# Attention turned on VectorE in 32x32 blocks, and its softmax moved behind the low part of u

## The reference, cut to what matters

```
out    = (q k^T * scale) v              # per head; no softmax over keys here
out    = softmax(out, axis=-1)          # over the 8 channels of a head
x      = x + concat_heads(out) @ wo^T + wo_b
t      = rms_norm(layer_norm(x))        # tokens for the experts
w      = top-2 of 8 experts, from softmax(t @ gate^T)
h1, h3 = t @ w1^T + lora1_e, t @ w3^T + lora3_e     # base shared, LoRA per expert, rank 16
act    = silu(h1) * h3
x      = x + sum_e w_e * (act @ w2^T + lora2_e)
```

## Time and profile before

| | us |
|---|---|
| three timed runs | 297.27, 297.6, 298.34; median 297.6 |
| span of the profiled execution, first to last instruction | 296.7 |
| between that span and the median | 0.9 |

### The profile page before, as it was taken

How to read it: one execution, slowest core, us unless ns; L and a number is a source line. 1 busy time by engine, 2 the same in 40 slices (tenths; PEclk the granted TensorE clock), 3 DMA queues, 4 the chain that set the end, 5 groups by cost and what they waited for, 6 DMA issues and landing times. The chain is left out here.

```text
span 296.7 us, 4518 instructions
## 1 busy us (share of the span) xinstructions
PE 287.4 (97%) x1487; PEld 238.4 (80%) x1487; DVE 221.4 (75%) x607; ACT 187.5 (63%) x310; POOL 187.0 (63%) x186
## 2 busy tenths in 40 slices
PE   8779999999999999999999999999999999999995
PEld 6557888878888888888888888888888887878874
DVE  3878986995689658894589765895579965795295
ACT  1467967674945966757755868459656658655532
POOL 3375599288970889419990589608982389518930
PEclk9979999999999999999999999999999999999999
DMA  5720020200220021200211011200012000200002
GB/s 147 287 66 9 0 73 1 72 1 11 97 73 0 0 72 38 71 1 2 71 50 60 0 49 59 71 0 2 1 37 73 0 0 35 75 1 0 0 2 71
DMA packets 7225, 12.45 MB, mean 42 GB/s; under 512 B 1825, under 2 KB 3234, under 8 KB 7202
## 3 DMA queue, kind: packets, MB, share of 16 engines
q1 hardware_dynamic: 6768, 11.77, 12.0%
q10 hardware_dynamic: 434, 0.39, 0.4%
HBM read 10.03 MB, written 2.13 MB: 41 GB/s over the span
## 5 line engine op out<-in xcount | busy, mean ns | idle before, releaser
L989 ACT ACTIVATE silu<-h_ps 128x512 f32<-128x512 f32 x64 | 37.4, 596 | 31.4 <-PE h_ps L641 29.8
L1639 POOL TENSOR_TENSOR um_lo<-umf,um_hi 128x1024 fp32r<-128x1024 f32 x7 | 16.9, 2414 | 60.5 <-ACT um_hi L981 60.5
L641 PE MATMUL h_ps<-um_hi,b_hi 128*128 128x512 f32 x128 | 51.4, 401 | 0.0
L641 PE MATMUL h_ps<-um_lo,b_hi 128*128 128x512 f32 x128 | 50.3, 393 | 0.5 <-DVE um_lo L1309 0.5
L641 PE MATMUL h_ps<-um_hi,b_lo 128*128 128x512 f32 x128 | 49.9, 390 | 0.0
L1322 DVE TENSOR_TENSOR act_first<-silu,h_ps 128x512 f32<-128x512 f32 x32 | 21.4, 680 | 20.9 <-ACT silu L989 16.1
L1322 DVE TENSOR_TENSOR act_second<-silu,h_ps 128x512 f32<-128x512 f32 x32 | 21.7, 679 | 16.6 <-PE h_ps L641 14.7
L1661 POOL TENSOR_TENSOR scaled<-act_second,ratio 128x512 f32<-128x512 f32 x24 | 31.5, 1313 | 1.3 <-DVE act_second L1322 1.3
L641 PEld LDWEIGHTS h_ps<-um_lo,b_hi 128*128 128x128 f32 x128 | 24.0, 188 | 6.9 <-DVE um_lo L1309 1.4
L981 ACT CAST um_hi<-umf 128x1024 fp32r<-128x1024 f32 x14 | 14.8, 1055 | 23.2 <-DVE umf L1303 22.2
L641 PEld LDWEIGHTS h_ps<-um_hi,b_lo 128*128 128x128 f32 x128 | 24.1, 188 | 4.5
(11 more groups left out here) (278 smaller groups left out, 789.2 us busy)
## 6 DMA issues: line engine op xcount, KB each, us to landing
chosen<-choice_dram SPq DMA_DIRECT2D x7, 512.0 KB, 3.6
x_in<-in_x_dram SPq DMA_DIRECT2D x7, 256.0 KB, 2.9
ctx_in<-in_ctx_t_dram SPq DMA_DIRECT2D x7, 256.0 KB, 3.2
out_dram<-y SPq DMA_DIRECT2D x7, 256.0 KB, 2.0
act_second<-in_hidden_w_dram SPq DMA_DIRECT2D x1, 512.0 KB, 4.1
act_second<-in_lora_w_dram SPq DMA_DIRECT2D x1, 512.0 KB, 5.6
v_parts<-in_down_w_dram SPq DMA_DIRECT2D x1, 512.0 KB, 5.3
ctx_in<-in_ctx_t_dram ACTq DMA_DIRECT2D x2, 128.0 KB, 3.2
```

Source lines behind the costliest of these rows:

```text
L641: mm = nc.tensor.matmul((h1_ps, h3_ps)[s][n % 2][:], b13[w][:, s, c * P:(c + 1) * P], um[k][m][:, s, :], start=False, stop=(i == 2), skip_ ...
L989: nc.scalar.activation(silu[:, n % SILU_RING, :], h1_ps[n % 2][:], ACT.Silu).then_inc(silu_done.sem, 1)
L1639: nc.gpsimd.tensor_tensor(um[1][1][:], umf[1][:], as_f32(um[1][0][:]), ALU.subtract)\
```

## The change

For the blocks n >= 2 (`AHEAD` = 2):

- `attention_out` swaps the operands of its matmuls, so that `b_ps` holds channels (heads) on partitions and tokens along the row.
- DVE's new `turn_o(n)` transposes each 32x32 square of `b_ps` into `heads` (SBUF); a group of 8 columns is then one head of one token. It stands where `top_of_o` and `shift_o` stood.
- `top_of_o` and `shift_o` read `heads` instead of PSUM and stand later: behind `um_low(b+1)` and `v_part(b, 0)`. `sum_exp` follows `v_part(b, 1)`.
- DVE's new `turn_heads(n)` transposes the 32x32 squares of `heads` back into `heads_t`, at the head of the next iteration, in front of `act_step(b, 0)`. PE's `turn_heads` and ACT's `heads_turned` go.
- ACT: `exp_o` stands behind `exp_ratio`. POOL: `norm_heads` stands behind `ctx_low`. The second matmul group on `b_ps` (`a2_product`, k = 1) waits for `turn_o` in place of `shift_o`, and `project` takes over the wait for the logits.

```diff
             def attention_out(n, i=WHOLE):
...
+                if n < AHEAD:
+                    by_tile(o_bank(n, i), queries, pairs, i=i).then_inc(o_mm.sem, 1)
+                else:
+                    by_tile(o_bank(n, i), pairs, queries, i=i).then_inc(o_mm.sem, 1)
...
                 hidden(b, 1)
-                turn_heads(b + 1)
...
-                        used = (ktv_done, o_shifted)[k]
-                        pe.wait_ge(used.sem, used.of(b + 2))
+                        if k == 0:
+                            pe.wait_ge(ktv_done.sem, ktv_done.of(b + 2))
+                        else:
+                            pe.wait_ge(o_turned, b + 3 - AHEAD)
...
                 v_high(b - 1)
-                heads_turned(b + 1)
...
                 um_high(b + 1, 1)
+                exp_ratio(b + 1)
                 if early:
                     exp_o(b + 2)
-                exp_ratio(b + 1)
...
+            def scores(n, i):
+                src = o_bank(n, i) if n < AHEAD else flat(heads)
+                return src[:].rearrange("p (g k) -> p g k", k=DK)[:, groups(i)]
+
+            def turn_o(n):
+                ve.wait_ge(o_mm.sem, o_mm.of(n))
...
+                nc.vector.transpose(flat(heads), o_bank(n, WHOLE)[:]).then_inc(o_turned, 1)
+
+            def turn_heads(n):
+                ve.wait_ge(heads_done.sem, heads_done.of(n))
+                ve.wait_ge(wo_mm.sem, wo_mm.of(n - 1))
+                nc.vector.transpose(heads_t[:], flat(heads)).then_inc(heads_t_done.sem, 1)
...
             def shift_o(n, i=WHOLE):
...
-                o = o_bank(n, i)[:].rearrange("p (g k) -> p g k", k=DK)[:, groups(i)]
+                o = scores(n, i)
                 top = top_o[:, groups(i)]
                 nc.vector.tensor_tensor(e_o[:, groups(i)], o, top.unsqueeze(2).to_broadcast([P, len(tiles(i)) * HEADS, DK]),
                                         ALU.subtract).then_inc(o_shifted.sem, 1)
...
             for b in range(1, LAST):
                 early = b + 2 < BLOCKS
+                turn_heads(b + 1)
                 act_step(b, 0)
...
                 if early:
-                    top_of_o(b + 2)
-                    shift_o(b + 2)
+                    turn_o(b + 2)
                 act_step(b, 7)
...
                 v_part(b, 0)
                 if early:
+                    top_of_o(b + 2)
+                    shift_o(b + 2)
+                v_part(b, 1)
+                if early:
                     sum_exp(b + 2)
-                v_part(b, 1)
                 first_weight(b + 1)
...
                 um_low(b + 1)
+                if b + 3 < BLOCKS:
+                    ctx_low(b + 3)
                 if early:
                     norm_heads(b + 2)
-                if b + 3 < BLOCKS:
-                    ctx_low(b + 3)
```

More of the change, by code:

```diff
@@ L290, in build_program @@
         top_o_done = signal("top_o_done", first=2)
+        o_turned = sem("o_turned")
         o_shifted = signal("o_shifted", first=2)
@@ L540, in attention_out @@
                 pe.wait_ge(ktv_done.sem, ktv_done.of(n, upto(i)))
-                by_tile(o_bank(n, i), lambda t: q_t[:, t * P:(t + 1) * P], lambda t: ktv[:, t, :], i=i)\
-                    .then_inc(o_mm.sem, 1)
+                queries, pairs = (lambda t: q_t[:, t * P:(t + 1) * P]), (lambda t: ktv[:, t, :])
+                if n < AHEAD:
+                    by_tile(o_bank(n, i), queries, pairs, i=i).then_inc(o_mm.sem, 1)
+                else:
+                    by_tile(o_bank(n, i), pairs, queries, i=i).then_inc(o_mm.sem, 1)
             def turn_heads(n, i=WHOLE):
@@ L547, in turn_heads @@
                     pe.wait_ge(umf_done.sem, umf_done.of(0))
-                elif n > 1:
-                    pe.wait_ge(logits_done.sem, logits_done.of(n - 1))
                 turn(heads_bank(n, i), lambda t: heads[:, t, :], i).then_inc(heads_t_mm.sem, 1)
@@ L554, in project @@
                     pe.wait_ge(wo_ready, 1)
+                elif n >= AHEAD:
+                    pe.wait_ge(logits_done.sem, logits_done.of(n - 1))
                 pe.wait_ge(heads_t_done.sem, heads_t_done.of(n, upto(i)))
@@ L1077, in _ @@
             z_high(0, 2)
-            exp_o(2)
             exp_ratio(1)
@@ L1082, in _ @@
             um_high(1, 1)
+            exp_o(2)
             for b in range(1, LAST):
@@ L1186, in mask_ktv @@
                     .then_inc(ktv_done.sem, 1)
-            def top_of_o(n, i=WHOLE):
-                ve.wait_ge(o_mm.sem, o_mm.of(n, upto(i)))
-                o = o_bank(n, i)[:].rearrange("p (g k) -> p g k", k=DK)[:, groups(i)]
+            def scores(n, i):
[3 more added lines that the diff above has]
+                ve.wait_ge(o_mm.sem, o_mm.of(n))
+                if n == AHEAD:
+                    ve.wait_ge(heads_t_mm.sem, heads_t_mm.of(n - 1))
+                else:
+                    ve.wait_ge(heads_t_done.sem, heads_t_done.of(n - 1))
+                nc.vector.transpose(flat(heads), o_bank(n, WHOLE)[:]).then_inc(o_turned, 1)
[3 more added lines that the diff above has]
+                nc.vector.transpose(heads_t[:], flat(heads)).then_inc(heads_t_done.sem, 1)
+            def top_of_o(n, i=WHOLE):
+                if n < AHEAD:
+                    ve.wait_ge(o_mm.sem, o_mm.of(n, upto(i)))
+                else:
+                    ve.wait_ge(o_turned, n + 1 - AHEAD)
+                o = scores(n, i)
                 nc.vector.tensor_reduce(top_o[:, groups(i)], o, AX_X, ALU.max).then_inc(top_o_done.sem, 1)
@@ L1482, in _ @@
             mask_ktv(2)
+            turn_o(2)
             act_step(0, 7)
-            top_of_o(2)
-            shift_o(2)
             b_low(0, 1)
@@ L1497, in _ @@
             um_low(1)
-            first_weight(1)
             v_part(0, 0)
+            top_of_o(2)
+            shift_o(2)
             v_part(0, 1)
             sum_exp(2)
+            first_weight(1)
             for b in range(1, LAST):
                 early = b + 2 < BLOCKS
+                turn_heads(b + 1)
                 act_step(b, 0)
```

## The result

The changed kernel takes 308.1 us (median of 4 runs, 306.8 to 308.2) against 298.0 for the kernel before: a ratio of 1.032, with a 95% interval of 1.029 to 1.034 (the two medians alone give 1.034). The forecast was 305.7 us, in a range of 300.5 to 310.5. The span of the profiled execution is 306.3 us, 9.6 more than before. PE is busy for 290.3 us of it (95%), where it was busy for 97% before.

A forecast was written before the change was run, and what follows sets the result against it. PE was taken as the bound, with a VectorE and ScalarE chain one microsecond behind. Delays of 6.05 and 2.01 raised the 296.7 span to 304.8; plus 0.9 gave 305.7 us, own range 303.5 to 307.5, set range 300.5 to 310.5.

The forecast's parts named there:

- shift_o held until um_lo's end plus 0.55: VectorE's shift_o, both inputs in SBUF, stands until POOL's um_lo ends and finishes 0.55 later, taking about 1.75 instead of 0.69.
- The second rival: shift_o is not held, its second input being only 64 columns read eight times: 1.7 lost, 299.3 us; chance 0.12.
- The chain exp_o, xn, table load, silu 0, act_first: ACT and VectorE work behind shift_o gives PE the h3 bank 1.10 late; with 0.11 weight load, 1.21 a block.
- the 1.4 of waiting: Sign: PE waits about 1.4 for act_first or silu before hidden step 2 in each of blocks 1 to 6.
- The turns give nothing while PE waits: PE's head turns cost 0.43 in each of blocks 2 to 7; without them PE only arrives sooner and waits longer.
- turn_o and turn_heads at 0.69: VectorE's new transposes take 0.69 each, adding nothing to the loss; range kept for turn_o 0.67 to 1.24.
- the first rival: turn_heads is held by POOL's v as well: 4.5 more in all, 310.2 us; chance 0.15.
- Block 6, 2.01: With no xn before silu, the heads decide: PE gets h3 1.90 late, 2.01 with the weight load.
- The sum, 8.1: Delayed starts of blocks 1 to 5, 6.05, plus block 6, 2.01: together 8.1 us more.
- The 0.9 outside the span: Added to the predicted span of 304.8, because the earlier runs' median was 0.9 above the profiled span of 296.7.
- Two inputs in SBUF: Rule used for shift_o: VectorE instructions with two SBUF inputs need the port pair that POOL locks for a whole instruction.
- the estimate of 1.24: VectorE transpose of 128x512 as four times the skill's 311 ns; it would make the sum 1.7 larger.

The follow-up runs named there:

- 1: Changed kernel, but in blocks 2 to 7 top_of_o writes its 64 columns to PSUM, so shift_o has one SBUF input: 300.7 us, ratio 1.009.
- 2: Changed kernel with both shift_o inputs in SBUF, but POOL's um_lo waits until shift_o is done and norm_heads precedes ctx_lo: 306.7 us.
- 3: Changed kernel with POOL's um_lo waiting for shift_o (both inputs in SBUF) and ctx_lo ahead of um_lo in POOL's order: 305.2 us.
- 4: Changed kernel with top_of_o and shift_o directly behind VectorE's um_lo, columns still in SBUF, and block 7's turn_heads later: 306.6 us.
- 7: Changed kernel with top_of_o's columns in PSUM, top_of_o and shift_o directly behind VectorE's um_lo, and block 7's turn_heads later: 297.7 us, ratio 0.997.
- 6: Changed kernel with only turn_heads of block 7 moved behind the second act_step of block 6: 307.2 us, ratio 1.030.

## Why the prediction was right, and what it mis-sized

- *shift_o held until um_lo's end plus 0.55, about 1.75 long:* right (1.74; 0.54 behind). The runs show it from both sides: 0.69 with one input in PSUM beside POOL (1), 0.69 with both in SBUF without POOL (2, 3), 2.33 when it stands sooner (4). The second rival falls: a second input of 64 columns is enough.
- *The chain exp_o, xn, table load, silu 0, act_first, and 1.21 a block:* right; 1.18 to 1.23 in blocks 2 to 5 and 1.14 in block 1. Of the 1.4 of waiting that were to show in front of hidden step 2, 1.13 do, 0.65 of them for xn and 0.48 for silu; the wait for act_first, which was to end last, shows only in block 6.
- *The turns give nothing while PE waits:* right. Where nothing is late (7), they give the 0.43 a block at which they were costed.
- *turn_o and turn_heads at 0.69, turn_heads not held:* 0.72 and 0.71, and not held beside POOL's v; the first rival falls.
- *Block 6, 2.01:* measured 1.8 up to the h3 bank, with a wait for silu (0.88) in front of the one for act_first (0.91).
- *The sum, 8.1:* its own terms came to 7.75 (5.97 in five blocks, 1.78 in block 6), and the span to 9.6 more. Not in the sum were the 0.44 by chance in the opening, and the 1.4 behind block 6. That two pauses of PE close together can cost more than their length was missing among the steps.
- *The 0.9 outside the span:* mis-sized, and it is 0.9 of the 2.4 us by which 305.7 is too low. In every run whose span is on record the time is 1.75 to 1.92 above the span of the same execution. The profiled execution before, with a span of 296.7, was one of the slower ones, and its span was taken together with the median of others.
- *The range:* 308.1 lies above 303.5 to 307.5, the forecast's own range. It is inside 300.5 to 310.5 because that range was drawn up to the first rival's 310.2, and this rival didn't come true. The mechanism was right; that the time fell inside is in part luck.

## What to carry to other kernels

When an operand moves from PSUM to SBUF, look at what POOL runs beside the pass that reads it, and price that pass by the end of POOL's instruction rather than by its own length; one small operand left in PSUM may undo most of it (7.4 of 10.1 us here). A move that removes a wait is judged by the next thing in each queue it passes: three of eight edits here (2, 3 and 6) did at their own place what they should and lost most of the gain to a new neighbour. An engine that has time on average has none where it stands at the head of a serial chain: VectorE was busy for 75% of the span before, and yet its 1.05 longer pass went through ACT's exponential, xn, table load and silu to PE.

## What the runs showed of the hardware that was not expected

- TENSOR_SCALAR on the mask, with one large input (bf16, in SBUF), was held by POOL as shift_o was: 1.77 in place of 0.72 (experiment 3). den, also a TENSOR_SCALAR, was held in the earlier trace rows, and where um_lo runs beside it (experiments 2 and 3) it takes 0.70 in the mean, 0.27 in the changed kernel. "Two inputs in SBUF", the step's wording, is thus too narrow. The Trainium skill, SBUF — State Buffer, section "SBUF: two separate sides", counts VectorE passes in a two-port performance mode among those that take the shared pair. Whether this pass runs in such a mode no run here shows: alone it takes 0.72, which is no shorter than shift_o's 0.69.
- VectorE's transposes of 128x512 f32 from SBUF to SBUF were not held: 0.71 in the mean of six, POOL's v beside them. The Trainium skill, VectorE: DVE Perf Modes, section "The three transpose paths", gives 311 ns for 128x128 bf16; the estimate of 1.24, four times that, is not what was measured.
- The granted clock fell to 0.50, the 1.2 GHz level, behind two waits of PE, 0.88 and 0.91, whose ends lie 1.9 us apart, and was at 1.00 again from 254. It stayed at 1.00 with one wait of 0.92 and one of 0.35 (experiment 6), and with one of 1.36 in block 6 (experiment 3). What exactly brings it down these runs don't settle.
